# First message layer of a graph network: the two halves of the scalar channel summed on TensorE instead of VectorE

## The chip, the cores and the metric

The kernel runs on one core of a Trainium2 chip. The metric is the device time of one execution in microseconds (us). The kernel before was timed in three runs, and one further execution was profiled; every row below is from that execution.

## The reference, cut to what matters

The program is a graph network of four layers on 6250 nodes with 256 features and 106250 edges. Only the first layer is touched. There, for each edge, four weights of 64 channels (`tpw`) come from a small network on the edge's 16 attributes, and a message of one scalar and three vector channels of 64 is formed from the sender's row and summed at the receiver:

```python
r = silu(silu(silu(edge_rbf @ M1) @ M2) @ M3)
tpw = (r @ M4).reshape(-1, 4, C)                    # C = 64
x0, x1 = up0[snd], up1[snd]
sh0, sh1 = edge_sh[:, 0], edge_sh[:, 1:]
m0e = tpw[:, 0] * x0 * sh0[:, None] + tpw[:, 3] * einsum("ecx,ex->ec", x1, sh1) * inv3
m1e = tpw[:, 1][:, :, None] * x0[:, :, None] * sh1[:, None, :] + tpw[:, 2][:, :, None] * x1 * sh0[:, None, None]
msg0 = segment_sum(m0e, rcv, n)
msg1 = segment_sum(m1e, rcv, n)
```

`m0e` is the scalar channel. Its two summands, and the two of `m1e`, are the halves that this case is about. The factor `inv3` is put into the last quarter of M4 once.

## The kernel before

The message stage is the function `convolve`. Edges are sorted by receiver and cut into 880 tiles of 128 edges (`ST`), each of which belongs to one tile of 128 receiving nodes. A batch is 8 tiles (`UC`), so there are 110 batches (`NBC`); each batch is worked in two halves `m` of 4 tiles. One batch ahead of the messages, TensorE, ScalarE and VectorE prepare what the next batch needs; the order on each engine is written out by hand in its `body`.

Per batch, the engines do this:

- GpSimd gathers the senders' rows, one indirect transfer a tile (L1109), into `rows`. A gather into a buffer waits for signal `x`, with which VectorE says that it has read the rows, and for `tp`.
- TensorE runs the small network for all 8 tiles at once: a transpose (L1196), the first layer (L1204, four products), the second and third layer (L1207, one product each). Its last layer (L1218, four products on 64 rows each) is done once a half into `psT`, and waits for the message signal `msg` of the half that used this part of `psT` before.
- ScalarE evaluates the layers' activations (L1126), scales the gathered rows by the three vector harmonics into `z` (L1138, 12 a half; slots 1 to 3 of `z` are the scalar feature times the harmonics, slots 4 to 6 the vector features times them), and scales two quarters of `psT` by the scalar harmonic into `tps` (L1147, 4 a half).
- VectorE builds `sel`, the one-hot matrices of the receivers, once a batch (L1277), and the messages of a half in `products`: it sums slots 4 and 5 of `z` (L1292), makes the three vector channels of half 1 of `prod` (L1295), adds slot 6 (L1297), makes the scalar channel of half 0 (L1298), multiplies the summed slot 0 of `z` by the last weight quarter (L1301), makes the vector channels of half 0 (L1302, whose signal `x` frees the rows), and adds the scalar channel's second half into half 0 (L1305, whose signal is `msg`).
- TensorE in `multiply` then sums the messages at the receivers, for each tile with two products of the one-hot matrix that accumulate in the same bank `psA`: half 0 with 256 columns (L1230: scalar and three vector channels), half 1 with the 192 columns of the vector channels only (L1233). Each product is two instructions in the trace. It waits for `msg`, and for VectorE to have emptied the bank.
- VectorE adds each tile's result to the sums of its node tile in `acc` (L1319), four times a half, each add after the one before.

VectorE's order in a batch is: products of half 0, the adds of the last batch's half 1, the selection for the next batch, products of half 1, the adds of half 0. TensorE's is: last layer of the next batch's half 0, multiply half 0, layers 3 and 1 of later batches, last layer of half 1, multiply half 1, layer 2, transpose. The signal `y` counts VectorE's own steps, four a half before; VectorE waits on it where one of its instructions reads what an earlier one wrote.

All the other stages (the edge sorting before it, the contraction after it, and three more layers) follow one another and don't share instructions with this one.

Of the kernel before, what the change touches and what calls it, by code (L numbers as in the profile page):

```python
# [9 lines left out]
ALU = mybir.AluOpType  # L10
# [17 lines left out]
C = 64  # L28
# [121 lines left out]
def reach(eng, sem, value):  # L150

    if not isinstance(value, int) or value > 0:
        eng.wait_ge(sem, value)
# [858 lines left out]
def convolve(nc, k, tag):  # L1012
# [8 lines left out]
    with es:  # L1021
        S = {n: s[tag + n] for n in names + gats}

        def sb(name, shape, dt=F32):
            return es.enter_context(nc.sbuf_tensor(tag + name, shape, dt))
# [8 lines left out]
        sel = [sb(f"sel{b}", [P, UC, P]) for b in range(2)]  # L1034
# [10 lines left out]
        prod = sb("prod", [P, 2, 2, 4, 4, C])  # L1045
# [8 lines left out]
        def batches(eng, body):  # L1054

            for t in range(2):
                body(t, t % 2, t // 2)
            with eng.Fori(1, NBC // 2 - 3) as i:
                for b in range(2):
                    body(i * 2 + b, b, i)  # L1060
            for t in range(NBC - 6, NBC):
                body(t, t % 2, t // 2)

        def is_one(t):
            return not isinstance(t, int) or t < NBC

        def place(n):

            return n % 2 * 2 + n // 2
# [5 lines left out]
        @block.sync  # L1075
        def _(sp):
            for b in range(2):
                sp.dma_start(idx[b][:, :], k.src_of[:, b * UC:(b + 1) * UC]).then_inc(i_sem[b], 16)
                rbf_load(sp, b, b)
            sp.wait_ge(S["wf"], 3)  # L1080
            for n in range(UC):
                sp.dma_start(m1[n * 16:(n + 1) * 16, n // 2, n % 2 * C:(n % 2 + 1) * C], k.w["M1"]).then_inc(S["w"], 16)

            def load(t, b, i):
                if later(i):
                    for m in range(2):
                        sp.wait_ge(g_sem[b][m], i * 64)
                    sp.dma_start(idx[b][:, :], k.src_of[:, ds(t * UC, UC)]).then_inc(i_sem[b], 16)
                if later(i):
                    sp.wait_ge(S["sk"], (t - 1) * 2)  # L1090
                sp.dma_start(sh[b][:, :, :], k.sh_steps[ds(t * UC, UC), :].rearrange("t (e f) -> e t f", f=4)
                             ).then_inc(ls_sem[b], 16)

            pairs(sp, NBC, load)
# [93 lines left out]
        @block.tensor  # L1188
        def _(pe):
            pe.wait_ge(S["w"], 16 * (UC + 6))  # L1190
            pe.wait_ge(S["wf"], 4)

            def turn(t, b, i):
                pe.wait_ge(lr_sem[b], i * 16 + 16)
                reach(pe, S["a3"], t - 1)
                nc.tensor.transpose(psM[:, b, 0:P], rbf[b][:, :, :].rearrange("p u f -> p (u f)"), k.ident[:, :]  # L1196
                                    ).then_inc(S["rt"], 1)

            def layer(q, t, b):
                before, out = (("rx", "m1"), ("a1", "m2"), ("a2", "m3"))[q - 1]  # L1200
                pe.wait_ge(S[before], t + 1)
                if q == 1:
                    for n in range(QB):
                        ins = nc.tensor.matmul(psM[:, b, n * P:(n + 1) * P], m1[:, n, :], rT[b][:, :],  # L1204
                                               start=True, stop=True)
                else:
                    ins = nc.tensor.matmul(psM[:, b, :], (m2, m3)[q - 2][:, :], (r1, r2)[q - 2][b][:, :],  # L1207
                                           start=True, stop=True)
                ins.then_inc(S[out], 1)

            def last_layer(t, b, m):
                if m == 0:
                    pe.wait_ge(S["a3"], t + 1)
                reach(pe, S["msg"], t * 2 + (m - 1))
                for q in range(2):
                    for u in range(2):
                        half = slice(u * C, u * C + C)
                        ins = nc.tensor.matmul(psT[:, m, u, q, :], r3[b][half, (2 * m + q) * P:(2 * m + q + 1) * P],  # L1218
                                               m4[half, :], start=True, stop=True)
                ins.then_inc(S["tp"], 1)  # L1220

            def multiply(t, b, m):
                pe.wait_ge(S["msg"], t * 2 + (m + 1))
                pe.wait_ge(S["sel"], t + 1)
                for q in range(2):
                    reach(pe, S["acc"], t * UC + (4 * m + 2 * q - 2))
                    for u in range(2):
                        n = 2 * q + u
                        out = psA[:, q, u, :]
                        nc.tensor.matmul(out, sel[b][:, 4 * m + n, :],  # L1230
                                         prod[:, m, 0, place(n), :, :].rearrange("p k c -> p (k c)"),
                                         start=True, stop=False)
                        ins = nc.tensor.matmul(out[:, C:], sel[b][:, 4 * m + n, :],  # L1233
                                               prod[:, m, 1, place(n), 1:4, :].rearrange("p k c -> p (k c)"),
                                               start=False, stop=True)
                    ins.then_inc(S["mm"], 1)

            for t in range(2):
                turn(t, t, 0)
            for q in range(1, 4):  # L1240
                for t in range(2):
                    layer(q, t, t)
            turn(2, 0, 1)
            turn(3, 1, 1)
            layer(1, 2, 0)
            layer(2, 2, 0)
            last_layer(0, 0, 0)
            last_layer(0, 0, 1)

            def body(t, b, i):  # L1250
                if is_one(t + 1):
                    last_layer(t + 1, 1 - b, 0)
                multiply(t, b, 0)
                if is_one(t + 2):
                    layer(3, t + 2, b)
                if is_one(t + 3):
                    layer(1, t + 3, 1 - b)
                if is_one(t + 1):
                    last_layer(t + 1, 1 - b, 1)
                multiply(t, b, 1)  # L1260
                if is_one(t + 3):
                    layer(2, t + 3, 1 - b)
                if is_one(t + 4):
                    turn(t + 4, b, i + 2)

            batches(pe, body)

        @block.vector
        def _(v):
# [11 lines left out]
            def products(t, b, i, m):  # L1281
                x = rows[b][:, m, :, :].rearrange("p n (k c) -> p n k c", c=C)
                tp = psT[:, m, :, :, :].rearrange("p u q (k c) -> p (u q) k c", c=C)
                zs = z[:, m, :, :, :]
                pr = prod[:, m, :, :, :, :]

                def three(t):
                    return t.unsqueeze(2).broadcast_to([P, 4, 3, C])

                scaled = tps[:, m, :, :, :]  # L1290
                v.wait_ge(S["z"], t * 2 + (m + 1))
                nc.vector.tensor_tensor(zs[:, :, 0, :], zs[:, :, 4, :], zs[:, :, 5, :], ALU.add).then_inc(S["y"], 1)  # L1292
                v.wait_ge(S["sk"], t * 2 + (m + 1))
                reach(v, S["mm"], t * 4 + (2 * m - 2))
                nc.vector.tensor_tensor(pr[:, 1, :, 1:4, :], three(tp[:, :, 1, :]), zs[:, :, 1:4, :], ALU.mult)  # L1295
                v.wait_ge(S["y"], t * 8 + (4 * m + 1))
                nc.vector.tensor_tensor(zs[:, :, 0, :], zs[:, :, 0, :], zs[:, :, 6, :], ALU.add).then_inc(S["y"], 1)  # L1297
                nc.vector.tensor_tensor(pr[:, 0, :, 0, :], scaled[:, :, 0, :], x[:, :, 0, :], ALU.mult  # L1298
                                        ).then_inc(S["y"], 1)
                v.wait_ge(S["y"], t * 8 + (4 * m + 2))  # L1300
                nc.vector.tensor_tensor(zs[:, :, 0, :], tp[:, :, 3, :], zs[:, :, 0, :], ALU.mult).then_inc(S["y"], 1)  # L1301
                nc.vector.tensor_tensor(pr[:, 0, :, 1:4, :], three(scaled[:, :, 1, :]), x[:, :, 1:4, :], ALU.mult  # L1302
                                        ).then_inc(S["x"], 1)
                v.wait_ge(S["y"], t * 8 + (4 * m + 4))
                nc.vector.tensor_tensor(pr[:, 0, :, 0, :], pr[:, 0, :, 0, :], zs[:, :, 0, :], ALU.add).then_inc(S["msg"], 1)  # L1305

            def tiles_of(at, n):
                return nc.values_load_multi_w_load_instructions(
# [1203 lines left out]
```

## Time and profile before

| | before |
|---|---|
| median of three runs | 5600.34 us (5598.19 to 5601.46) |
| profiled execution | 5590.46 us |
| its span, first to last instruction | 5588.70 us |
| message stage of the first layer, VectorE's first selection to its last add | 171.2 to 1456.4 us (starts) |

The profile lists, for the whole program, busy times and costliest groups of instructions. "PEld" is TensorE's weight load, which overlaps its products, "PE" the products. A busy time of PE is modelled, since products are pipelined; in the timeline the starts of successive instructions are the firmer reading. "Idle before" is the time for which the engine stood idle ahead of an instruction, and the arrow names what ended most of it; "issue" means that the profile shows nothing that it waited for. The granted clock is a share of TensorE's full speed.

### The profile page before, as it was taken

Reading aid. Unit: us, or ns where it says so; the run is one execution under the profiler, and the core shown is the slowest. Engines: PE = TensorE matmul, PEld = TensorE weight load, DVE = VectorE, ACT = ScalarE, POOL = GpSimd, SP = SyncE. Lnnn points to the kernel's source line nnn. Section 1 sums busy time; section 2 is a strip of 40 time slices with the busy share of each in tenths; the row PEclk is TensorE's granted clock in tenths of the full one; section 3 lists DMA queues with packets and bytes.
Section 4 is the critical chain, followed back from the end, with each engine's and each line's share of the span. In section 5 each row is a group of like instructions: output and inputs, shape, how many; then the busy total and the mean of one; then the engine's idle time right before and its main releaser. Section 6 shows DMA issues by size and latency. Waiting matters only on the chain. (4 is left out here: it accounts for less than half of the span.)

```text
span 5588.7 us, 88640 instructions
## 1 busy us (share of the span) xinstructions
PE 3899.8 (70%) x21179; PEld 3037.0 (54%) x21180; DVE 4054.8 (73%) x9127; ACT 2969.4 (53%) x8461; POOL 3608.6 (65%) x3623
## 2 busy tenths in 40 slices
PE   4799999999766666666684556555575566555666
PEld 3577777777545555555463455544433455454552
DVE  4799999999763333333376888888876788888887
ACT  4799999999554444444362333333343333333332
POOL 2577777777317777777607777777701777777760
PEclk9899999999877888888786777777787777777777
DMA  8444444444225455455325555555502555555543
GB/s 270 109 98 98 99 98 99 98 99 98 69 64 136 135 135 135 134 134 134 106 98 147 144 145 146 146 145 141 145 15 84 144 144 144 144 140 142 144 119 95
DMA packets 693372, 687.44 MB, mean 123 GB/s; under 512 B 458792, under 2 KB 561755, under 8 KB 691471
## 3 DMA queue, kind: packets, MB, share of 16 engines
q0 software_dynamic: 173552, 491.76, 30.9%
q1 hardware_dynamic: 378451, 164.47, 11.7%
q10 hardware_dynamic: 141276, 30.14, 2.8%
q8 instruction: 39, 0.64, 0.0%
q14 instruction: 54, 0.44, 0.0%
HBM read 627.87 MB, written 57.66 MB: 123 GB/s over the span
## 5 line engine op out<-in xcount | busy, mean ns | idle before, releaser
L1935 POOL DMA_INDIRECT g3rows<-sender_rows,g3idx x880 | 847.1, 963 | 515.0 <-issue 261.3
L1109 POOL DMA_INDIRECT c0rows<-rows,c0idx x880 | 994.8, 1130 | 285.2 <-issue 271.5
L1935 POOL DMA_INDIRECT g2rows<-sender_rows,g2idx x880 | 847.2, 963 | 399.3 <-issue 274.5
L878 POOL DMA_INDIRECT g1rows<-rows,g1idx x880 | 833.5, 947 | 350.4 <-issue 264.0
L999 DVE TENSOR_TENSOR acc<-acc,g1psA 128x258 f32 x660 | 279.7, 424 | 723.0 <-PE g1psA L904 568.5
L1138 ACT ACTIVATE c0z<-c0rows,c0sh 128x128 f32<-128x128 f32 x2640 | 795.3, 407 | 1.7 <-DMA c0rows<-rows,c0idx 1.7
L907 PE MATMUL g1psA<-g1rows,g1sel 128*128 128x129 f32 x2640 | 474.8, 348 | 359.0 <-DMA g1rows<-rows,g1idx 321.6
L907 PEld LDWEIGHTS g1psA<-g1rows,g1sel 128*128 128x128 f32 x2640 | 455.1, 259 | 402.1 <-issue 348.0
L1969 PE MATMUL g3psA<-g3rows,g3sel 128*128 128x136 f32 x2640 | 440.6, 327 | 157.3 <-DVE g3rows L2147 102.5
L1230 PE MATMUL c0psA<-c0prod,c0sel 128*128 128x256 f32 x1760 | 547.6, 393 | 3.5 <-DVE acc L1319 3.5
L1969 PE MATMUL g2psA<-g2rows,g2sel 128*128 128x132 f32 x2640 | 439.1, 327 | 155.0 <-DVE g2rows L2147 102.3
L1969 PEld LDWEIGHTS g3psA<-g3rows,g3sel 128*128 128x128 f32 x2640 | 408.0, 230 | 232.1 <-issue 110.5
L1969 PEld LDWEIGHTS g2psA<-g2rows,g2sel 128*128 128x128 f32 x2640 | 408.8, 234 | 227.1 <-issue 108.4
L1233 PE MATMUL c0psA<-c0prod,c0sel 128*128 128x192 f32 x1760 | 430.6, 326 | 0.0
L1319 DVE TENSOR_TENSOR acc<-acc,c0psA 128x256 f32 x880 | 367.1, 417 | 25.8 <-PE c0psA L1233 3.2
L932 ACT ACTIVATE g1fT<-g1psF 128x512 f32<-128x512 f32 x104 | 62.1, 597 | 573.4 <-PE g1psA L904 573.4
L1233 PEld LDWEIGHTS c0psA<-c0prod,c0sel 128*128 128x128 f32 x1760 | 335.1, 190 | 45.8
L1230 PEld LDWEIGHTS c0psA<-c0prod,c0sel 128*128 128x128 f32 x1760 | 298.9, 190 | 76.5 <-DVE acc L1319 51.4
L2163 DVE TENSOR_TENSOR acc<-acc,g3psA 128x272 f32 x660 | 286.6, 434 | 19.7 <-PE g3psA L1966 2.5
L2163 DVE TENSOR_TENSOR acc<-acc,g2psA 128x264 f32 x660 | 280.6, 425 | 20.0 <-PE g2psA L1966 2.5
L2037 ACT ACTIVATE g2al<-g2arg 128x2 f32<-128x2 f32 x55 | 11.2, 203 | 508.7 <-DVE g2arg L2119 508.7
L947 ACT ACTIVATE g1sel<-iota,dst_in 128x128 f32<-128x128 f32 x880 | 267.7, 389 | 9.6 <-PEq L80 5.1
(432 smaller groups left out, 8735.0 us busy)
## 6 DMA issues: line engine op xcount, KB each, us to landing
g2bc<-dst_rows SPq DMA_DIRECT2D x55, 512.0 KB, 3.9
g3bc<-dst_rows SPq DMA_DIRECT2D x55, 512.0 KB, 3.9
g1f<-in_edge_attr SPq DMA_DIRECT2D x103, 256.0 KB, 3.5
c0rows<-rows,c0idx POOLq DMA_INDIRECT x880, 2.8
g1rows<-rows,g1idx POOLq DMA_INDIRECT x880
g2rows<-sender_rows,g2idx POOLq DMA_INDIRECT x880
g3rows<-sender_rows,g3idx POOLq DMA_INDIRECT x880
rbf_steps<-prep_extra POOLq DMA_DIRECT2D x7, 1024.0 KB, 10.7
```

Source lines behind the costliest of these rows:

```text
L878: g.indirect_dma_start(rows[b][:, u, 0:D], None, k.table, bass.IndirectOffsetOnAxis(ap=idx[b][:, u:u + 1], axis=0)).then_inc(r_sem[b], 16)
L907: ins = nc.tensor.matmul(to[:, o, n * HALF:(n + 1) * HALF], sel[b][:, u, :], rows[b][:, u, o * HALF:(o + 1) * HALF], start=True, stop=True)
L947: ins = nc.scalar.activation(sel[b][:, u, :], k.iota[:, :], ACT.Abs, bias=k.dst_in[:, ds(t * U2 + u, 1)], scale=-1.0)
L999: ins = nc.vector.tensor_tensor(to, to, of[:, 0:2, n * HALF:(n + 1) * HALF], ALU.add)
L1109: g.indirect_dma_start(rows[b][:, m, place(n), :], None, k.table, bass.IndirectOffsetOnAxis(ap=idx[b][:, 4 * m + n:4 * m + n + 1], axis=0) ...
L1138: ins = nc.scalar.activation(z[:, m, place(n), 1 + x:5 + x:3, :], row[:, 0:2 + x:1 + x, :], ACT.Copy, scale=sh[b][:, 4 * m + n, 1 + x:2 + x])
L1230: nc.tensor.matmul(out, sel[b][:, 4 * m + n, :], prod[:, m, 0, place(n), :, :].rearrange("p k c -> p (k c)"), start=True, stop=False)
L1233: ins = nc.tensor.matmul(out[:, C:], sel[b][:, 4 * m + n, :], prod[:, m, 1, place(n), 1:4, :].rearrange("p k c -> p (k c)"), start=False, ...
L1319: ins = nc.vector.tensor_tensor(to, to, psA[:, q, u, :], ALU.add)
L1935: g.indirect_dma_start(rows[b][:, u, 0:TW], None, k.sender_rows, bass.IndirectOffsetOnAxis(ap=idx[b][:, u:u + 1], axis=0)).then_inc(gas[b] ...
L1969: ins = nc.tensor.matmul(to[:, o, n * HALF:(n + 1) * HALF], sel[:, u, :], rows[b][:, u, o * HALF:(o + 1) * HALF], start=True, stop=True)
L2163: ins = nc.vector.tensor_tensor(to, to, of[:, 0:2, n * HALF:(n + 1) * HALF], ALU.add)
```

## The change

Half 1 of the scalar channel is written to its own place in `prod`, slot 0 of half 1, which was unused. The second product of each tile (L1233) takes 256 columns instead of 192 and writes the whole bank, so TensorE accumulates the two scalar halves as it does the vector halves. VectorE's sum L1305 is dropped; the product L1301 moves behind L1302, writes `prod` instead of `z`, and now carries the signal `msg`. The signal `y` counts two steps a half instead of four.

```diff
-                        ins = nc.tensor.matmul(out[:, C:], sel[b][:, 4 * m + n, :],
-                                               prod[:, m, 1, place(n), 1:4, :].rearrange("p k c -> p (k c)"),
+                        ins = nc.tensor.matmul(out, sel[b][:, 4 * m + n, :],
+                                               prod[:, m, 1, place(n), :, :].rearrange("p k c -> p (k c)"),
                                                start=False, stop=True)
...
-                v.wait_ge(S["y"], t * 8 + (4 * m + 1))
+                v.wait_ge(S["y"], t * 4 + (2 * m + 1))
                 nc.vector.tensor_tensor(zs[:, :, 0, :], zs[:, :, 0, :], zs[:, :, 6, :], ALU.add).then_inc(S["y"], 1)
-                nc.vector.tensor_tensor(pr[:, 0, :, 0, :], scaled[:, :, 0, :], x[:, :, 0, :], ALU.mult
-                                        ).then_inc(S["y"], 1)
-                v.wait_ge(S["y"], t * 8 + (4 * m + 2))
-                nc.vector.tensor_tensor(zs[:, :, 0, :], tp[:, :, 3, :], zs[:, :, 0, :], ALU.mult).then_inc(S["y"], 1)
+                nc.vector.tensor_tensor(pr[:, 0, :, 0, :], scaled[:, :, 0, :], x[:, :, 0, :], ALU.mult)
                 nc.vector.tensor_tensor(pr[:, 0, :, 1:4, :], three(scaled[:, :, 1, :]), x[:, :, 1:4, :], ALU.mult
                                         ).then_inc(S["x"], 1)
-                v.wait_ge(S["y"], t * 8 + (4 * m + 4))
-                nc.vector.tensor_tensor(pr[:, 0, :, 0, :], pr[:, 0, :, 0, :], zs[:, :, 0, :], ALU.add).then_inc(S["msg"], 1)
+                v.wait_ge(S["y"], t * 4 + (2 * m + 2))
+                nc.vector.tensor_tensor(pr[:, 1, :, 0, :], tp[:, :, 3, :], zs[:, :, 0, :], ALU.mult).then_inc(S["msg"], 1)
```

## Rows read from the trace of the kernel before

**Rows 1.** Busy us by stretch of the span, with granted clock and DMA.

```profile
core 0: us, PE busy (x) PEld busy (x) DVE busy (x) ACT busy (x) POOL busy (x), PEclk, DMA share, GB/s
200.00:400.00 200.00, 198.03 (x1061) 153.06 (x1061) 195.42 (x399) 191.10 (x627) 156.19 (x138) 1.00 0.43 97
...
1200.00:1400.00 200.00, 197.97 (x1062) 153.22 (x1062) 195.68 (x402) 190.98 (x627) 157.64 (x140) 1.00 0.43 99
```

**Rows 2.** Groups, 300 to 1300 us: count, busy us, mean ns, idle before, releasers.

```profile
L1319 DVE TENSOR_TENSOR acc<-acc,c0psA 128x256 f32 x696 | 290.3, 417 | 17.9
...
L1218 PEld LDWEIGHTS c0psT<-c0m,c0r 64*128 64x128 f32 x1392 | 119.8, 186 | 80.0 <-DVE c0prod L1305 72.2
L1277 DVE TENSOR_TENSOR c0sel<-iota,dst_in 128x1024 f32<-128x1024 f32 x87 | 105.9, 1218 | 0.0
L1204 PE MATMUL c0psM<-c0rT,c0m 128*128 128x128 f32 x696 | 91.7, 275 | 0.0
...
L1305 DVE TENSOR_TENSOR c0prod<-c0prod,c0z 128x256 f32<-128x256 f32 x174 | 73.6, 423 | 0.0
```

**Rows 3.** Timeline of VectorE, two batches from 704.90: start us, us, instruction.

```profile
704.90 1.77 DVE L1319 TENSOR_TENSOR acc<-acc,c0psA 128x256 f32 x4
...
708.46 0.41 DVE L1301 TENSOR_TENSOR c0z<-c0psT,c0z 128x256 f32<-128x256 f32 x1
708.79 0.95 DVE L1302 TENSOR_TENSOR c0prod<-c0tps,c0rows 128x768 f32<-128x768 f32 x1
709.66 0.47 DVE L1305 TENSOR_TENSOR c0prod<-c0prod,c0z 128x256 f32<-128x256 f32 x1
710.05 1.77 DVE L1319 TENSOR_TENSOR acc<-acc,c0psA 128x256 f32 x4
...
716.00 0.41 DVE L1305 TENSOR_TENSOR c0prod<-c0prod,c0z 128x256 f32<-128x256 f32 x1
716.33 1.77 DVE L1319 TENSOR_TENSOR acc<-acc,c0psA 128x256 f32 x4
...
727.94 0.41 DVE L1319 TENSOR_TENSOR acc<-acc,c0psA 128x256 f32 x1
```

**Rows 4.** Timeline of TensorE's products, one batch from 705.03.

```profile
705.03 1.14 PE L1218 MATMUL c0psT<-c0m,c0r 64*128 64x256 f32 x8 [0.17 <-DVE c0prod L1305]
706.10 0.70 PE L1230 MATMUL c0psA<-c0prod,c0sel 128*128 128x256 f32 x2
706.63 0.49 PE L1233 MATMUL c0psA<-c0prod,c0sel 128*128 128x192 f32 x2
706.96 0.59 PE L1230 MATMUL c0psA<-c0prod,c0sel 128*128 128x256 f32 x2
707.39 0.49 PE L1233 MATMUL c0psA<-c0prod,c0sel 128*128 128x192 f32 x2
...
709.23 1.02 PE L1207 MATMUL c0psM<-c0r,c0m 128*128 128x512 f32 x2
710.09 0.27 PE L1196 MATMUL c0psM<-ident,c0rbf 128*128 128x128 f32 x1
710.29 1.13 PE L1218 MATMUL c0psT<-c0m,c0r 64*128 64x256 f32 x8
...
715.34 1.05 PE L1204 MATMUL c0psM<-c0rT,c0m 128*128 128x128 f32 x8
716.46 0.91 PE L1218 MATMUL c0psT<-c0m,c0r 64*128 64x256 f32 x5
```

**Rows 5.** Timeline of VectorE and TensorE in the stage's last batches.

```profile
1429.60 0.41 DVE L1305 TENSOR_TENSOR c0prod<-c0prod,c0z 128x256 f32<-128x256 f32 x1
...
1430.06 1.14 PE L1218 MATMUL c0psT<-c0m,c0r 64*128 64x256 f32 x8 [0.97 <-DVE c0prod L1305]
...
1431.13 0.30 PEld L1230 LDWEIGHTS c0psA<-c0prod,c0sel 128*128 128x128 f32 x2 [0.33 <-issue]
...
1440.97 0.41 DVE L1305 TENSOR_TENSOR c0prod<-c0prod,c0z 128x256 f32<-128x256 f32 x1
```

## The prediction

> **What bounds the kernel now.** Only one of the kernel's stages is touched, the message stage of the first layer, so I read that stage alone. I began with the busy times by stretch. In six stretches of 200 us between 200 and 1400 us, all alike, TensorE shows 198 us busy, VectorE 195, ScalarE 191, GpSimd 156 to 158, and the granted clock is 1.00 throughout, which is the 2.4 GHz level [rows 1] (the first and the last of the six stand there). Three engines are nearly full, so shares don't say who sets the pace; the waits and the starts have to.
>
> The grouped rows of 1000 us count the batches: the selection L1277 runs once a batch and 87 times, so **a batch takes 1000 / 87 = 11.49 us**, and the last sum L1305 runs twice a batch [rows 2]. There VectorE's groups have no releaser behind their idle time (17.9 us before the 696 adds of L1319, nothing before L1305), while TensorE's weight loads of L1218 wait 72.2 us for VectorE's L1305 [rows 2]. VectorE's timeline says the same: each instruction starts before the one ahead has ended, and two batches take 727.94 - 704.90 = 23.04 us, 11.52 each [rows 3]. **VectorE sets the pace**, and TensorE arrives early twice a batch. The question is how early.
>
> For that, TensorE's timeline from one L1218 to its second successor, by differences of starts [rows 4]: L1218 1.07, four tiles of L1230 and L1233 3.13, L1207 0.86, the transpose L1196 0.20, L1218 1.06, the second half's tiles and L1207 from 711.35 to 715.34 = 3.99 (711.35 is 710.29 + 1.06), L1204 1.12; together 11.43. Which of these are work? L1204 issues eight matmuls in 1.05 us, the last of which lasts 0.275 [rows 2, 4]; so they start (1.05 - 0.275) / 7 = 0.111 apart, and the eight are issued in 0.886. The rest of its 1.12, 0.23, is waiting: VectorE's L1305 begins at 716.00, lasts 0.41, and L1218 starts at 716.46, 0.05 after its end [rows 3, 4]. The transpose hands over in its own 0.20. So TensorE needs 11.43 - 0.23 = **11.20 us a batch**, and against the mean of 11.49 it has **0.29 us spare**. VectorE, the bound, is only 2.6% ahead of it.
>
> **What the change removes.** L1305, 128x256 on VectorE, goes: 220 instructions, two a batch. Their mean duration is 0.423 [rows 2], but the successor starts earlier: 716.00 to 716.33 is 0.33, 709.66 to 710.05 is 0.39 [rows 3]. I take 0.335 (the neighbouring L1301 to L1302 shows 0.33 as well), so VectorE's batch falls by 0.67 to 11.49 - 0.67 = **10.82 us**. The product L1301 is not removed: it moves behind L1302 and writes the empty first slot of prod instead of z, same shape, same operands, so I price the move at nothing. Its wait on the second sum of L1297 is then three instructions old instead of one. The two semaphore increments that go with it carry no busy time in any row. Their cover is VectorE's new slack; without it they'd cost at most what separates the starts, 0.33.
>
> Signals move too. The message signal comes 0.33 earlier in VectorE's chain, the signal that frees the gathered rows (after L1302) also 0.33 earlier. Behind the latter wait GpSimd's gathers; GpSimd is 156 of 200 us busy, 9.0 us of an 11.49 us batch [rows 1], so an earlier release is worth nothing and can start no collision that a DMA share of 0.43 [rows 1] would feel. No wait is added on any engine, and no DMA is touched.
>
> **What the change adds.** L1233 takes 256 columns instead of 192: 880 tiles, two instructions each. Its new shape is already in the trace, as L1230: from L1230's start to L1233's is 0.43 (706.96 to 707.39), from L1233's to the next L1230 0.33 (706.63 to 706.96); over tiles, (709.23 - 706.96) / 3 = 0.757 less 0.43 is 0.325 [rows 4]. 0.43 / 256 and 0.325 / 192 are both 1.7 ns, so time goes by columns, and the weight loads beside them are hidden already at 192. The price is **0.105 us a tile**, 0.84 a batch, 92 us over 880 tiles. It can't be below this while the clock stands at 1.00; from above, nothing in the rows makes it dearer.
>
> **The sum.** TensorE would need 11.20 + 0.84 = **12.04 us**, VectorE 10.82, ScalarE 191 / 200 of 11.49 = 10.97, GpSimd 9.0. TensorE becomes the bound by over a microsecond, and a batch grows by 12.04 - 11.49 = 0.55. What becomes late next is VectorE's add (L1319) and ScalarE's activations, which now wait for TensorE; ScalarE has 1.07 us and VectorE 1.22 us of slack to absorb that. There are 110 batches; in the last three the layers of the small network (L1204, L1207) have run out, TensorE sits idle 0.97 us before L1218, and VectorE still sets the pace (1429.60 to 1440.97 is 11.37) [rows 5]. So 107 x 0.55 = +59 us, and about -2 us at the end (three batches at 0.67 less): **+57 us**. The profiled execution took 5590.46 us, 1.76 more than its span of 5588.70; it would become 5647.5. The median of the runs shown is 5600.34, 9.9 above that execution, so I forecast 5600.34 + 57 = **5657 us**, +1.0%.
>
> The uncertain term is TensorE's spare time. **Upper bound**: none of the 0.29 is regained, because L1204's 1.12 belongs to a change to the 64-row products that follow; then 107 x 0.84 - 2 = +88, 5688 us. **Lower bound**: gaps close that I counted as work. L1218's four products of 256 columns take 1.07 before the next group, where two at a time at 0.43 would be 0.86; and the first tile takes 706.10 to 706.96 = 0.86 instead of 0.757 [rows 4]. That is 0.21 + 0.10 = 0.31 a half, 0.62 a batch. If a third closed, 107 x 0.21 = 22 us would come off: +35, 5635 us. I take the value without either: L1196 gives way to L1218 in its own 0.20, so the change to 64 rows costs nothing there; and in the drained end, where TensorE has just stood idle, L1230's weight load still comes 1.07 after L1218's start (1430.06 to 1431.13), with issue and no other engine named ahead of it [rows 5], so that gap is no waiting for VectorE.
>
> **Rivals.**
> 1. *The spare time is not regained* (5688 us). For it: L1204 to L1218 is TensorE's only such transition, and no row shows it without a wait. Against: the start 0.05 us behind L1305's end, twice in these rows (716.46, and 1430.06 after 1429.60 + 0.41) [rows 3 to 5], shows it tied to VectorE.
> 2. *TensorE's busy time misleads, the columns are free* (faster). A busy matmul row includes the tail of pipelined work. Weight loads are busy 153 of 200 us [rows 1]; if that were TensorE's true load, VectorE's 0.67 would be gained in full: 110 x 0.67 = 74 us, 5527 us. It ends below the old time once TensorE's true need is under 11.49 - 0.84 = 10.65 us now, and in full under 9.98. Against it stand start times, not busy times: the intervals grow with columns. The Trainium skill, Perfetto Trace Analysis, section Identifying the Most-Contended Engine, says that matmul busy time is a poor measure of TensorE and that the share of weight loads is to be used instead; by that rule this is the case to expect, and the starts in [rows 4] speak against applying it here.
> 3. *The gaps close* (no change). With products ready early, TensorE's queue runs ahead and loads weights across the change of row groups; if 0.53 of the 0.62 us a batch vanished, the result would be 5600 us. The drained end speaks against it [rows 5].
> That the change wouldn't do what it says I leave out: the shapes are explicit in the code.
>
> **How the numbers follow.** The forecast (5635 to 5675) gets 0.69, the first rival 0.19, a slowdown above it, by an ordering among the three near-full engines that I don't see, 0.02; the free columns 0.05, closing gaps 0.05. For 8 in 10, the range goes from the lower bound, a little widened, to the first rival with 5 us of scatter: 5632 to 5693. A measurement of this kernel can tell about 0.2% (11 us) from no change. Faster 0.05, same 0.05, slower 0.90.
>
> **What would show it.** Right: VectorE's groups in 300 to 1300 us idle with TensorE as releaser, some 10% of the time; the waits of L1218 and its weight loads for VectorE gone; L1277 about 83 times in 1000 us; L1233 to L1230 at 0.43; the stage's last add some 57 us later, and every later stage unchanged. Wrong: L1277 87 times or more, or a VectorE that is still without idle time (rivals 2 and 3); L1204 to L1218 still over 1.08 with no wait shown (rival 1); a granted clock under 1.00 in the stage.

## The result: TensorE became the bound, and the profile after

The changed kernel took 5658.92 us (median of four runs, 5655.47 to 5660.56) against 5599.26 us for the kernel before on the same chip: ratio 1.0107, 95% interval 1.0089 to 1.0124, or 50 to 69 us slower. The forecast was 5657.

| | before | after |
|---|---|---|
| median | 5599.26 us | 5658.92 us |
| profiled execution / its span | 5590.46 / 5588.7 us | 5659.67 / 5657.7 us |
| message stage, first selection to start of the last add | 171.2 to 1456.4 = 1285.2 us | 171.8 to 1522.8 = 1351.0 us |
| batch in mid-stage | 23.04 / 2 = 11.52 us [rows 3] | 12.15 us |

The stage is 65.8 us longer, the profiled spans differ by 69.0, the medians by 59.7. The stage's own length is the cleanest of the three: it leaves out what the other stages do from run to run (it is read from one profiled execution of each kernel), and the profiled execution of before lay 9 us under its median. It is read from the start times of two lines of the changed kernel (duration ns min/median/max, first and last start us; L1316 is the add that was L1319):

```profile
L1277 DVE TENSOR_TENSOR c0sel<-iota,dst_in x110: 1212/1218/1220, 171.8 to 1503.8; 128x1024 f32<-128x1024 f32 x110
L1316 DVE TENSOR_TENSOR acc<-acc,c0psA x880: 402/420/423, 195.7 to 1522.8; 128x256 f32 x176
```

Busy us by stretch, columns as in [rows 1], kernel after:

```profile
200.00:400.00 200.00, 200.00 (x1006) 152.02 (x1004) 174.99 (x346) 182.70 (x594) 131.41 (x132) 1.00 0.39 93
...
1200.00:1400.00 200.00, 200.00 (x1005) 152.02 (x1003) 175.84 (x347) 182.82 (x595) 131.59 (x133) 1.00 0.39 94
```

TensorE's products have gone from 198 to 200 of 200 us, VectorE has fallen from 195 to 175, and the granted clock is 1.00, the 2.4 GHz level, as before. The groups of 300 to 1300 us show where VectorE now waits (columns as in [rows 2]; L1299 and L1302 are the last two products):

```profile
L1233 PE MATMUL c0psA<-c0prod,c0sel 128*128 128x256 f32 x1316 | 391.4, 379 | 0.0
...
L1218 PE MATMUL c0psT<-c0m,c0r 64*128 64x256 f32 x1320 | 187.2, 402 | 0.0
...
L1295 DVE TENSOR_TENSOR c0prod<-c0psT,c0z 128x768 f32<-128x768 f32 x165 | 157.8, 956 | 103.0 <-ACT c0tps L1147 103.0
...
L1277 DVE TENSOR_TENSOR c0sel<-iota,dst_in 128x1024 f32<-128x1024 f32 x83 | 101.1, 1218 | 0.0
```

L1218's products no longer wait, the selection runs 83 times instead of 87, and VectorE stands idle 124 us of the 1000 (busy 876), 103 of them before L1295; 17.0 lie before its adds, as 17.9 did before. The engine named ahead of L1295 is ScalarE, but ScalarE is only the messenger. The rows of one such wait, all engines (a timeline lists start us, us, instruction):

```profile
1479.97 1.13 PE L1218 MATMUL c0psT<-c0m,c0r 64*128 64x256 f32 x8
...
1485.45 1.05 PE L1204 MATMUL c0psM<-c0rT,c0m 128*128 128x128 f32 x8
...
1486.55 0.60 ACT L1126 ACTIVATE c0r<-c0psM 128x512 f32<-128x512 f32 x1 [0.29 <-PE c0psM L1204]
1487.04 1.14 ACT L1147 ACTIVATE c0tps<-c0psT,c0sh 128x128 f32<-128x128 f32 x4
...
1488.21 0.96 DVE L1295 TENSOR_TENSOR c0prod<-c0psT,c0z 128x768 f32<-128x768 f32 x1 [1.34 <-ACT c0tps L1147]
```

By the kernel's order this L1147 reads what the L1218 at 1479.97 made, 7 us earlier. It starts late because ScalarE's written order puts it behind the activation L1126, which waits for TensorE's L1204. So TensorE holds VectorE up by way of ScalarE. TensorE's products of one batch, kernel after:

```profile
702.59 1.13 PE L1218 MATMUL c0psT<-c0m,c0r 64*128 64x256 f32 x8
703.65 0.70 PE L1230 MATMUL c0psA<-c0prod,c0sel 128*128 128x256 f32 x2
704.19 0.59 PE L1233 MATMUL c0psA<-c0prod,c0sel 128*128 128x256 f32 x2
704.62 0.59 PE L1230 MATMUL c0psA<-c0prod,c0sel 128*128 128x256 f32 x2
705.05 0.59 PE L1233 MATMUL c0psA<-c0prod,c0sel 128*128 128x256 f32 x2
...
707.21 1.02 PE L1207 MATMUL c0psM<-c0r,c0m 128*128 128x512 f32 x2
708.07 1.05 PE L1204 MATMUL c0psM<-c0rT,c0m 128*128 128x128 f32 x8
709.05 1.13 PE L1218 MATMUL c0psT<-c0m,c0r 64*128 64x256 f32 x8
...
713.67 1.02 PE L1207 MATMUL c0psM<-c0r,c0m 128*128 128x512 f32 x2
714.53 0.27 PE L1196 MATMUL c0psM<-ident,c0rbf 128*128 128x128 f32 x1
714.74 1.14 PE L1218 MATMUL c0psT<-c0m,c0r 64*128 64x256 f32 x8
```

Set against [rows 4]: no row carries a wait; L1233 to L1230 is 704.62 - 704.19 = 0.43, was 0.33; the four tiles take 707.21 - 703.65 = 3.56, were 3.13; L1204 hands over to L1218 in 709.05 - 708.07 = 0.98, was 1.12; the whole batch, 702.59 to 714.74, is 12.15.

### The profile page after: what moved, and what is told of

Same layout as the page of the kernel before. It is cut to its first block and busy times, and to the rows that moved or that the text cites. A ratio compares the mean times of both kernels' runs of the same rounds, so it can differ in the third digit from the quotient of the medians.

```text
span 5657.7 us, 87910 instructions
## 1 busy us (share of the span) xinstructions
PE 3982.8 (70%) x21179; PEld 3085.3 (55%) x21180; DVE 3988.9 (71%) x8907; ACT 2980.9 (53%) x8461; POOL 3480.8 (62%) x3623
## 5 line engine op out<-in xcount | busy, mean ns | idle before, releaser
L1109 POOL DMA_INDIRECT c0rows<-rows,c0idx x880 | 878.5, 998 | 466.3 <-issue 342.7
L1230 PE MATMUL c0psA<-c0prod,c0sel 128*128 128x256 f32 x1760 | 546.8, 392 | 1.9 <-DVE acc L1316 1.9
L1233 PE MATMUL c0psA<-c0prod,c0sel 128*128 128x256 f32 x1760 | 523.8, 379 | 0.0
L1316 DVE TENSOR_TENSOR acc<-acc,c0psA 128x256 f32 x880 | 367.3, 417 | 25.6 <-PE c0psA L1233 3.0
L1230 PEld LDWEIGHTS c0psA<-c0prod,c0sel 128*128 128x128 f32 x1760 | 316.6, 190 | 109.4 <-issue 38.8
L1233 PEld LDWEIGHTS c0psA<-c0prod,c0sel 128*128 128x128 f32 x1760 | 334.7, 190 | 45.6
L1295 DVE TENSOR_TENSOR c0prod<-c0psT,c0z 128x768 f32<-128x768 f32 x220 | 210.3, 956 | 137.5 <-ACT c0tps L1147 137.5
```

The costliest lines, as they stand in the source:

```text
L1109: g.indirect_dma_start(rows[b][:, m, place(n), :], None, k.table, bass.IndirectOffsetOnAxis(ap=idx[b][:, 4 * m + n:4 * m + n + 1], axis=0) ...
L1230: nc.tensor.matmul(out, sel[b][:, 4 * m + n, :], prod[:, m, 0, place(n), :, :].rearrange("p k c -> p (k c)"), start=True, stop=False)
L1233: ins = nc.tensor.matmul(out, sel[b][:, 4 * m + n, :], prod[:, m, 1, place(n), :, :].rearrange("p k c -> p (k c)"), start=False, stop=True)
L1316: ins = nc.vector.tensor_tensor(to, to, psA[:, q, u, :], ALU.add)
```

## The experiments

The theory to be tested: TensorE's columns alone set the new time, with a threshold, since TensorE first uses up what it had spare. With the unhindered 0.98 from the trace after, TensorE's need before the change is 0.20 + 0.98 + 2 x 0.86 + 2 x 1.06 + 2 x 3.13 = 11.28 us a batch, against 11.51 to 11.52 that VectorE needed. The main rival: the slowdown sits in VectorE's new order, in which L1295 waits for ScalarE. The four kernels below were timed in the same series, with the kernel before at 5593.71 us.

### VectorE's part alone

```diff
-                        ins = nc.tensor.matmul(out, sel[b][:, 4 * m + n, :],
-                                               prod[:, m, 1, place(n), :, :].rearrange("p k c -> p (k c)"),
+                        ins = nc.tensor.matmul(out[:, C:], sel[b][:, 4 * m + n, :],
+                                               prod[:, m, 1, place(n), 1:4, :].rearrange("p k c -> p (k c)"),
```

> The changed kernel, but TensorE's second product keeps 192 columns; the scalar channel's second half is made by VectorE and left out of the sum. VectorE's share of the change is thus in alone. Theory (TensorE's columns set the new time): TensorE needs 0.20 + 0.98 + 2 x 0.86 + 2 x 1.06 + 2 x 3.13 = 11.28 us a batch, which is the bound, VectorE 10.84; against 11.51 before that is 107 x 0.23 = 25 us less than the kernel before, about 5575 us, with L1277 about 88 to 89 times in 300 to 1300 us. Rival (the slowdown sits in VectorE's new order and the later hand-over from ScalarE that L1295 waits for): no column is added, the order stays, so it remains near 5659 us. Rival (VectorE alone set the time before): 110 x 0.67 = 74 us less, about 5525 us.

Measured: 5564.52 us, ratio 0.9946 (0.9932 to 0.9959), 29 us under the kernel before. The stage runs from 173.1 to 1432.2, 1259.1 us, 26.1 less. Groups of 300 to 1300 us, then TensorE's timeline:

```profile
L1295 DVE TENSOR_TENSOR c0prod<-c0psT,c0z 128x768 f32<-128x768 f32 x177 | 168.9, 954 | 35.7 <-ACT c0tps L1147 35.7
...
L1277 DVE TENSOR_TENSOR c0sel<-iota,dst_in 128x1024 f32<-128x1024 f32 x88 | 107.2, 1219 | 0.0
...
L1218 PEld LDWEIGHTS c0psT<-c0m,c0r 64*128 64x128 f32 x1416 | 121.9, 186 | 61.4 <-DVE c0prod L1302 42.9
```

```profile
701.76 1.13 PE L1218 MATMUL c0psT<-c0m,c0r 64*128 64x256 f32 x8
...
706.81 1.05 PE L1204 MATMUL c0psM<-c0rT,c0m 128*128 128x128 f32 x8
707.80 1.14 PE L1218 MATMUL c0psT<-c0m,c0r 64*128 64x256 f32 x8
...
713.05 1.13 PE L1218 MATMUL c0psT<-c0m,c0r 64*128 64x256 f32 x8
```

A batch is 713.05 - 701.76 = 11.29, TensorE's need to within 0.01. So the slowdown doesn't sit in VectorE's new order: the same order, with L1295 waiting 35.7 us for ScalarE, is faster than the kernel before. And VectorE's relief of 0.67 a batch brings only 11.52 - 11.29 = 0.23, because TensorE stands right behind it. One row warns: L1218's weight loads still show 42.9 us of waiting for VectorE, though the product itself always starts 0.98 to 0.99 after L1204 (707.80 - 706.81 here). The weight load's idle time lies beside streaming products; of the 72.2 us in [rows 2], too, only some 20 (0.23 in each of 87 batches) were lost time.

### TensorE's part alone

```diff
-                        ins = nc.tensor.matmul(out[:, C:], sel[b][:, 4 * m + n, :],
-                                               prod[:, m, 1, place(n), 1:4, :].rearrange("p k c -> p (k c)"),
+                        ins = nc.tensor.matmul(out, sel[b][:, 4 * m + n, :],
+                                               prod[:, m, 1, place(n), :, :].rearrange("p k c -> p (k c)"),
...
             pe.wait_ge(S["wf"], 4)
+            pe.wait_ge(S["cl"], 2)
...
+            nc.vector.memset(prod[:, :, 1, :, 0, :], 0.0).then_inc(S["cl"], 1)
             nc.vector.memset(k.acc[:, :, 0:D], 0.0).then_inc(S["cl"], 1)
```

The first add of the stage waits for the second count of `cl`, too.

> The kernel before, VectorE's sum and order untouched, but the second product takes 256 columns; the added 64 read a place that is set to zero once, so they add nothing to the result. TensorE's share of the change is in alone. Theory: TensorE needs 12.15 us a batch as in the changed kernel, VectorE 11.51, so the same time as the changed kernel within 10 us, about 5660 us, L1277 82 to 83 times in 300 to 1300 us, and VectorE idle about 5% of the stretch. Rival (VectorE's order is the cause): the time of before, 5600 us. Rival (both parts matter): 5700 us and more, since VectorE's work is back while TensorE's is in.

Measured: 5664.9 us, ratio 1.0123 (1.0108 to 1.0139), which overlaps the changed kernel's 1.0089 to 1.0124. The stage runs from 171.2 to 1525.1, 1353.9 us; the changed kernel's took 1351.0. Groups of 300 to 1300 us (the edit shifts the lines: L1279 is the selection, L1297 the product that reads `psT` first, L1307 the sum that the change drops):

```profile
L1297 DVE TENSOR_TENSOR c0prod<-c0psT,c0z 128x768 f32<-128x768 f32 x164 | 156.5, 954 | 44.7 <-ACT c0tps L1147 44.7
...
L1279 DVE TENSOR_TENSOR c0sel<-iota,dst_in 128x1024 f32<-128x1024 f32 x83 | 101.1, 1218 | 0.0
L1307 DVE TENSOR_TENSOR c0prod<-c0prod,c0z 128x256 f32<-128x256 f32 x165 | 72.0, 436 | 0.0
```

83 selections, as in the changed kernel, with all of VectorE's work still there; its idle time before the first product that reads `psT` is 44.7 us instead of 103.0, and the difference of 58 us is about the sum that it still makes. Once the columns are in, VectorE's relief is worth 2.9 us of the stage. Mid-stage batches are alike in both kernels (12.15 us; from 703.14 to 715.29 here), so these 2.9 lie in the first batches and the drained end. The slowdown is the columns.

### The change in one half of each batch

```diff
-                        ins = nc.tensor.matmul(out, sel[b][:, 4 * m + n, :],
-                                               prod[:, m, 1, place(n), :, :].rearrange("p k c -> p (k c)"),
+                        wide2 = m == 1
+                        ins = nc.tensor.matmul(out if wide2 else out[:, C:], sel[b][:, 4 * m + n, :],
+                                               prod[:, m, 1, place(n), 0 if wide2 else 1:4, :].rearrange(
+                                                   "p k c -> p (k c)"),
```

`products` does the same: for the first half the order and the sum of before, for the second the order of the changed kernel.

> The change in the second of each batch's two halves only; the first half is as before (sum on VectorE, 192 columns). Theory (a threshold: the first 0.23 us a batch of added columns are free): TensorE 11.28 + 4 x 0.105 = 11.70 us a batch, VectorE 11.51 - 0.34 = 11.17; 107 x 0.19 = 20 us above the kernel before, about 5620 us, L1277 85 to 86 times in 300 to 1300 us. Rival (time goes with the columns from the first on): half of the whole change, 30 us, 5630 us.

Measured: 5624.27 us (5613.33 to 5628.76), ratio 1.0051 (1.0037 to 1.0065), 21 to 36 us above the kernel before. The rival's 30 lies in the middle of that interval and the theory's 20 just below it, so the median leans to the rival. But it counts the other stages too, which together took 4303.5 to 4314.9 us in the six profiled executions (span less stage). The stage itself tells more, by the selection's first start and the last add's, and by TensorE's rows of one batch:

```profile
L1279 DVE TENSOR_TENSOR c0sel<-iota,dst_in x110: 1212/1218/1221, 173.3 to 1461.5; 128x1024 f32<-128x1024 f32 x110
...
L1329 DVE TENSOR_TENSOR acc<-acc,c0psA x880: 401/420/423, 197.8 to 1480.9; 128x256 f32 x176
```

```profile
711.08 1.13 PE L1218 MATMUL c0psT<-c0m,c0r 64*128 64x256 f32 x8
...
722.80 1.13 PE L1218 MATMUL c0psT<-c0m,c0r 64*128 64x256 f32 x8
```

1480.9 - 173.3 = 1307.6 us, 22.4 more than before. A cost that goes with the columns from the first on would have made half of 65.8, or 33; the theory's threshold made 20. The batch says the same: 722.80 - 711.08 = 11.72, where the theory has 11.70 and the rival 11.52 + 0.63 / 2 = 11.83. The spans, 5622.5 and 5588.7, differ by 33.8 us; the other 11 lie outside the stage and aren't explained.

### Past the crossing: 128 columns

```diff
-                        ins = nc.tensor.matmul(out, sel[b][:, 4 * m + n, :],
-                                               prod[:, m, 1, place(n), :, :].rearrange("p k c -> p (k c)"),
+                        ins = nc.tensor.matmul(out[:, 2 * C:], sel[b][:, 4 * m + n, :],
+                                               prod[:, m, 1, place(n), 2:4, :].rearrange("p k c -> p (k c)"),
```

> The changed kernel with 128 columns in the second product; the scalar channel's and the first vector channel's second half are left out of the sum. Theory: TensorE needs 12.15 - 8 x 0.21 = 10.46 us a batch and is no longer the bound; then it is ScalarE with its 10.97, or VectorE with 10.84, and the batch stops falling there: 107 x 0.54 = 58 to 107 x 0.67 = 72 us under the kernel before, 5528 to 5542 us, VectorE or ScalarE without idle time. Rival (TensorE's columns set the time all the way): 10.46 us a batch, 112 us under the kernel before, 5488 us.

Measured: 5515.69 us, ratio 0.9861 (0.9846 to 0.9876), 78 us under the kernel before; the stage, 172.6 to 1380.1, is 77.7 shorter, 0.71 a batch over 110 batches. The rival's 112 is out. Groups of 300 to 1300 us, and busy times (columns as in [rows 1]):

```profile
L1295 DVE TENSOR_TENSOR c0prod<-c0psT,c0z 128x768 f32<-128x768 f32 x185 | 175.9, 951 | 0.0
...
L1218 PE MATMUL c0psT<-c0m,c0r 64*128 64x256 f32 x1480 | 209.9, 402 | 22.0 <-DVE c0prod L1302 18.7
```

```profile
300.00:1300.00 1000.00, 978.02 (x5639) 739.03 (x5638) 976.90 (x1941) 993.01 (x3328) 774.15 (x739) 1.00 0.45 105
```

The waits have changed sides again: VectorE has no idle time with a releaser (19.1 us before its adds, as before the change, and 4.0 before L1292), and TensorE waits for it. The batch is 11.52 - 0.71 = 10.81 us, which is VectorE's 10.82 of the prediction, so the new order adds nothing to VectorE's batch. The gain is a little above the expected 58 to 72: the batches of the drained end gain as well, and a batch fell by 0.71, not 0.67. The lower end, 58, rested on ScalarE's 10.97, which was no floor: ScalarE does its batch in 10.81 here, at 993 of 1000 us busy.

## Why the prediction was right, point by point

**The bound before** was read rightly. VectorE set the pace, with TensorE 0.23 us behind: the run without added columns gains just that and stops.

**The price of the columns**, 0.105 us a tile, was right, since the wider shape already stood in the trace: 0.43 between starts after the change, 12.15 - 11.29 = 0.86 a batch against 0.84 forecast. Nothing of it was hidden beyond the spare time.

**The spare time** is the mis-sized term: forecast 0.29, measured 11.52 - 11.29 = 0.23. I had counted 0.886 for the eight small instructions of L1204 up to the next L1218; without any wait it is 0.98 to 0.99 in all four kernels in which TensorE sets the pace (709.05 - 708.07 above). The upper bound of the prediction named this place and took 1.12; the truth lay between. I had ruled the extra out because the transpose hands over to the same products "in its own 0.20", but that 0.20 was not its own. In the kernel before, eight transposes of the same shape in the next stage, where the granted clock is 1.00 as well (1469.00 to 1470.20), start (1.09 - 0.272) / 7 = 0.117 apart (0.272 is the shortest duration of one):

```profile
1469.06 1.09 PE L1412 MATMUL t0psT<-ident,acc 128*128 128x128 f32 x8
```

So the transpose's 0.20 holds an extra of some 0.08. L1204's last instruction takes the same 0.20 to the next start (0.98 - 7 x 0.111), so the row that I took as evidence against rival 1 spoke for a part of it. By the measured terms the sum is 107 x (12.15 - 11.52) - 2 = 65 us, and the stage grew by 65.8. That the median came out at +59.7, closer to the forecast's 57, is luck: scatter of the rest of the program rather than a better sum, and its interval of 50 to 69 holds both.

**VectorE's relief** of 0.67 a batch was right in size (10.82 forecast, 10.81 reached with 128 columns; by the durations of the two sums, 2 x 0.423, it would have been 0.85) and worth almost nothing here: putting the sum back costs 2.9 us. Its idle time before L1295 came out at 10.3%, where some 10% was forecast, but the place and the releaser were wrong. The prediction had VectorE's add become late; the add's idle time stayed at 17 us. It also had ScalarE's activations wait for TensorE, and they do: L1126 stood idle 79.4 us of the 1000 where it was 38.9. That wait reaches VectorE's L1295 by way of L1147, which comes behind L1126 on ScalarE.

**ScalarE's need** of 10.97 was worked out as busy share times batch. It did no harm to the forecast, where TensorE's 12.04 lay far above, but as a floor it was wrong (10.81 with 128 columns).

**The rivals.** Spare time that isn't regained would have made 88 us; 65.8 is nearer to the forecast, with part of the rival in it. Gaps that close did not happen: L1218 to L1230 is 1.06 in the rows after, as before. The columns were not free. On that rival the Trainium skill, Perfetto Trace Analysis, section Identifying the Most-Contended Engine, holds that the share of weight loads (beside the arithmetic done against the peak) tells TensorE's headroom better than the products' busy time. Here that share was 153 of 200 us before [rows 1] and 152 after, when TensorE had become the bound; the products' 198 and 200 came nearer to the truth, and start-to-start intervals told it. The measurement decides against the share of weight loads as a measure for this stage.

**What was not tried.** VectorE's part alone gains 29 us, so a place for the sum that is neither VectorE nor TensorE could beat both kernels if it cost nothing there; that is not shown. ScalarE was 972 of 1000 us busy in that run. GpSimd, with 708 gathers, had 780 us busy and 221 us of short gaps ahead of them in the same 1000 us, so no free stretch shows in its rows. I put the sum on neither.

## What to carry to other kernels

Before work is moved from a full engine to another, work out how much the receiving engine needs when nothing holds it up, from differences of starts and not from busy shares or idle columns; the gain is the relief, or the spare time less the price of what is added, whichever is smaller. Here the relief was 0.67 us a batch, and the spare time of 0.23 less a price of 0.86 is a loss of 0.63. Where an added shape already runs elsewhere in the same trace, its price can be read there: 0.105 us a tile read, 0.86 / 8 = 0.107 paid.

## What the runs showed of the hardware that I had not expected

- The eight instructions of L1204 (128 columns and 128 rows each), followed by products on 64 rows, take 0.98 us to the next start, where their own spacing of 0.111 makes 0.886: the last one takes 0.20. A transpose ahead of the same 64-row products takes 0.20 to 0.21 where nothing waits (714.53 to 714.74 after), against a spacing of 0.117 among transposes. Why the hand-over takes longer was not tried.
- An engine at 95% busy can have more room than its share says: ScalarE's batch of 10.97 us by busy share (191 of 200 us) was done in 10.81.
- TensorE's time went by columns at clock 1.00: from L1233's start to the next L1230's it is 0.22, 0.33 and 0.43 for 128, 192 and 256 columns, about 1.7 ns a column.
